# A decoder layer on one core: the 8 x 128 maxima of each attention head turned by the array's transposition, where a float32 product with the identity turned them

## The chip, the cores and the metric

The kernel runs on one core of one Trainium2 chip. The metric is the time of one execution on the device in microseconds (us). Three runs of the kernel before gave 1570.14, 1571.79 and 1575.17 us. A further execution was profiled, and its rows are what is quoted here.

## What is computed

A post-norm decoder layer on x of shape (4, 1024, 256), all in float32. The parts, in order: an autocorrelation attention, a cross attention to 64 context rows, and a feed-forward part that is itself a self-attention with 16 heads of width 16 and a mixture of 8 experts. The change lies in that self-attention:

```python
        attn = jnp.einsum('bhnd,bhmd->bhnm', q, k) * (1.0 / np.sqrt(DK))
        attn = jax.nn.softmax(attn, axis=-1)
        y = jnp.einsum('bhnm,bhmd->bhnd', attn, v)
```

with n and m running over 1024 tokens, 4 batches and 16 heads, so 64 heads in all.

## The kernel before

The stage of the change is `project_and_attend`. It projects q, k and v, and then goes through 64 heads in slots, software-pipelined: in slot s four things of four heads are in flight.

- `a(k)`, eight a slot, for head s: scores of 128 queries against all 1024 keys, queries on the partitions (L307). VectorE takes their maxima, one `TENSOR_REDUCE` for each k (L548), into `sb_m_mx`, 128 partitions x 8.
- `maxima()`, once a slot, for head s - 1: the 128 x 8 maxima are turned to 8 x 128 in a PSUM bank (L364). ScalarE copies them out (L483), GpSimd splits them into three bf16 parts (L228 to L232), and the sync queue's DMA puts these as three further rows under q (L181), so that the next product subtracts the maxima by itself.
- `b(m, h)`, sixteen a slot, for head s - 2: scores again with keys on the partitions, maxima subtracted (L336). ScalarE takes the exponential of each (L470).
- `products(m0, lag)`, four a slot: exponentials times v and a column of ones (L351, float32).
- `results()`, once a slot, for head s - 3: the result is turned back (L377).

Nearly all of this is written for quarters of the array. The stationary operand has 32 columns, and four such products, for PSUM partitions 0, 32, 64 and 96, stand one after another in the code. In the trace such a product reads `96*32`, `99*32` or `128*32` (rows * columns of the stationary operand), and a product on the whole array reads `128*128`. Below, the quarter of PSUM partitions 0 to 31 is called the first quarter. The maxima are `128*8` and go to PSUM partitions 0 to 7, so to the first quarter alone.

The order within a slot is written out by hand. Around the change it is:

```python
                a(0), b(0, 0), b(0, 1), a(1), b(1, 0)
                products(6, 3)
                maxima()
                b(1, 1), b(2, 0), a(2), a(3), b(2, 1), b(3, 0)
                products(0, 2)
```

Slots 0 and 1 are different. They hold the last batch's projections (L259 and L273, on the whole array, `128*128`) between the `a(k)`, and in slot 1 `maxima()` stands after `a(2)` and ahead of an L273. From slot 2 to slot 63 every slot is full. Slot 64 and those behind it have no `a(k)` any more.

A float32 product stands in the trace as two pairs of a weight load (`PEld`) and a `MATMUL`, a bf16 product as one pair. The kernel already has other float32 transpositions on the whole array (`pe.transpose` in L245, L1306, L2433 and elsewhere).

Of the kernel before, what the change touches and what calls it, by code (L numbers as in the profile page):

```python
# [18 lines left out]
P = 128  # L19
TPB = S // P  # L20
# [21 lines left out]
def project_and_attend(nc, ctx, t, dram):  # L42
# [8 lines left out]
    def sb(name, shape, dt=F32):  # L51
        return ctx.enter_context(nc.sbuf_tensor("sb_m_" + name, shape, dt))

    def sem(name):
        return ctx.enter_context(nc.semaphore("m_" + name))
# [7 lines left out]
    ps, pz, ident, v_all, y_all = t["ps"], t["pz"], t["ident"], t["v_all"], t["y_all"]  # L63
# [7 lines left out]
    mx = sb("mx", [P, 2, TPB])  # L71
# [24 lines left out]
    def v_ready(b):  # L96
# [5 lines left out]
    set_up, v_in, scores1, maxed, mxT_done, mxT_read, split_done = (sem(n) for n in (  # L102
        "set_up", "v_in", "scores1", "maxed", "mxT_done", "mxT_read", "split_done"))
# [11 lines left out]
    def rotating(use):  # L115
        return 4 + ROTATION.index(use) % 3

    def maxima_bank(s):

        return ps[7] if s == 1 else ps[rotating("mxT")]  # L120
# [14 lines left out]
    with nc.Block() as block:  # L135
# [101 lines left out]
        def _(pe):  # L237
# [51 lines left out]
            def slot(s, par, it, edge):  # L289
# [66 lines left out]
                def maxima():  # L356
                    if not after:
                        return
                    pe.wait_ge(maxed, TPB * s)
                    if two:  # L360
                        pe.wait_ge(exped, W * e + FREE["mxT"])
                    elif s == 1:
                        pe.wait_ge(rest_done, U * B)
                    pe.matmul(maxima_bank(s)[0:TPB, 0:P], mx[:, (par - 1) % 2, :],  # L364
                              ident[:, :], start=True, stop=True).then_inc(mxT_done, 1)

                def results():
                    if not three:
# [20 lines left out]
                if s == 1:  # L389
                    for k in range(TPB):  # L390
                        values(B - 1, k)
                        a(k)
                        if k == 2:
                            maxima()
                    return
# [5 lines that stand above are left out]
# [2277 lines left out]
```

## Time and profile before

| what | value |
|---|---|
| time, three runs | 1570.14, 1571.79, 1575.17 us |
| the profiled execution: its time / span of its profile | 1574.36 / 1572.4 us |
| TensorE busy (share of the span) | 1501.7 us (96%) |
| VectorE busy | 1134.4 us (72%) |
| ScalarE busy | 879.7 us (56%) |
| GpSimd busy | 379.6 us (24%) |
| granted TensorE clock, mean | 0.986 |
| first and last maxima turned (L364) | at 468.4 and 1165.8 us of the span |

The span is the time from the first to the last instruction in the profile, and the execution's own time is 2.0 us longer. "PE busy" counts a matmul from its start to its modelled end, and neighbouring matmuls overlap, so the step from one start to the next tells more than the duration of one.

### The profile page before, as it was taken

The numbers are of one execution on the slowest core, as the hardware profiler recorded it, in microseconds if no ns is written. First come the engines' busy times: TensorE is split into PE (matmuls) and PEld (weight loads), VectorE is DVE, ScalarE is ACT, GpSimd is POOL, SyncE is SP. The second block draws the span as 40 slices with busy tenths as digits, with TensorE's granted clock in tenths as the row PEclk, the third lists the DMA queues.
The fourth block names the chain that finished last, engine by engine and source line by source line (L and its number), as shares of the span: only waits on it lengthen the run. The fifth ranks groups of instructions, "written<-read, shape, count | busy, mean of one in ns | idle before, by whom it ended". The sixth has DMA issues, their size and how long they took to land. (4 is left out here: it accounts for less than half of the span.)

```text
span 1572.4 us, 45249 instructions
## 1 busy us (share of the span) xinstructions
PE 1501.7 (96%) x18762; PEld 1107.1 (70%) x18762; DVE 1134.4 (72%) x1703; ACT 879.7 (56%) x1608; POOL 379.6 (24%) x604
## 2 busy tenths in 40 slices
PE   7999999978899999999999999999998999999997
PEld 4656677655445666666666666666657889999997
DVE  5787798876868898988889898988855633333332
ACT  2223666654447888888888888888884311111111
POOL 4110332223431111111111111111111125454443
PEclk9999999998999999999999999999999989999999
DMA  6000000002341111111111111111105945656552
GB/s 203 1 21 11 11 2 2 2 1 78 107 159 42 43 35 43 36 41 38 39 39 38 41 36 43 35 42 37 39 13 157 284 161 204 201 194 212 186 214 67
DMA packets 80082, 124.12 MB, mean 79 GB/s; under 512 B 22243, under 2 KB 46949, under 8 KB 79878
## 3 DMA queue, kind: packets, MB, share of 16 engines
q1 hardware_dynamic: 74262, 105.87, 22.3%
q0 software_dynamic: 5616, 15.34, 2.6%
q8 instruction: 151, 2.47, 0.7%
q14 instruction: 53, 0.43, 0.1%
HBM read 94.66 MB, written 26.08 MB: 77 GB/s over the span
## 5 line engine op out<-in xcount | busy, mean ns | idle before, releaser
L548 DVE TENSOR_REDUCE sb_m_mx<-banks 128x1 f32<-128x1024 f32 x512 | 603.5, 1219 | 76.6 <-PE banks L307 68.7
L470 ACT ACTIVATE sb_m_pT<-banks 128x512 f32<-128x512 f32 x1024 | 556.4, 595 | 110.4 <-PE banks L336 99.4
L336 PE MATMUL banks<-sb_m_q,sb_m_k 99*32 99x512 bf16 x4096 | 467.2, 380 | 2.1 <-DMA sb_m_q<-sb_m_mx_parts 1.2
L307 PE MATMUL banks<-sb_m_k,sb_m_q 96*32 96x512 bf16 x4096 | 360.1, 379 | 0.8 <-DVE sb_m_mx L548 0.5
L351 PE MATMUL banks<-sb_m_pT,sb_m_v 128*32 128x256 f32 x4096 | 314.8, 378 | 0.7 <-ACT sb_m_pT L470 0.7
L336 PEld LDWEIGHTS banks<-sb_m_q,sb_m_k 99*32 99x32 bf16 x4096 | 178.0, 95 | 81.0 <-ACT sb_m_pT L470 6.1
L351 PEld LDWEIGHTS banks<-sb_m_pT,sb_m_v 128*32 128x32 f32 x4096 | 176.2, 109 | 59.8 <-ACT sb_m_pT L470 1.2
L307 PEld LDWEIGHTS banks<-sb_m_k,sb_m_q 96*32 96x32 bf16 x4096 | 158.5, 96 | 76.3 <-DVE sb_m_mx L548 5.6
L2484 ACT ACTIVATE sb_e_hT<-banks 128x512 f32<-128x512 f32 x78 | 46.6, 597 | 236.8 <-PE banks L2442 236.8
L228 POOL CAST sb_m_mx_parts<-sb_m_mxT 8x128 bf16<-8x128 f32 x64 | 18.1, 284 | 574.4 <-issue 563.5
L2442 PEld LDWEIGHTS banks<-sb_e_xT,w 128*128 128x128 f32 x1248 | 145.3, 192 | 3.4 <-DVE sb_e_xT L2494 1.5
L2442 PE MATMUL banks<-sb_e_xT,w 128*128 128x128 f32 x1248 | 145.8, 275 | 1.1 <-DVE sb_e_xT L2494 1.1
L2459 PE MATMUL banks<-w,sb_e_hT 128*128 x624 | 141.2, 379 | 0.6 <-DVE sb_e_x L2501 0.6
L2459 PEld LDWEIGHTS banks<-w,sb_e_hT 128*128 128x128 f32 x624 | 115.5, 190 | 15.1 <-issue 1.0
L2501 DVE TENSOR_TENSOR sb_e_x<-sb_e_x,banks 128x256 f32<-128x256 f32 x39 | 16.4, 421 | 106.8 <-PE banks L2459 106.8
L2494 DVE TENSOR_SCALAR sb_e_xT<-banks,table_ln_w,table_ln_b 128x128 f32<-128x128 f32 x78 | 28.4, 406 | 56.5 <-PE banks L2433 56.5
L1453 DVE RECIPROCAL sb_b_rec<-banks 128x256 f32<-128x256 f32 x32 | 56.1, 1754 | 16.5 <-PE banks L1317 16.1
L780 PE MATMUL banks<-sb_w_qk,sb_xfT 128*128 128x512 f32 x128 | 57.3, 596 | 0.8 <-ACT sb_xfT L889 0.8
L377 PE MATMUL banks<-ident_sb,sb_m_y_raw 128*32 128x128 f32 x1024 | 56.9, 278 | 0.5 <-ACT sb_m_y_raw L478 0.5
L2405 POOL DMA_INDIRECT out_x<-sb_e_y,token_to x39 | 40.6, 1040 | 51.1 <-DVE sb_e_y L2515 49.6
L1407 ACT ACTIVATE sb_b_prT<-banks 128x1024 f32<-128x1024 f32 x32 | 32.8, 1023 | 33.4 <-PE banks L1306 33.4
L1240 POOL TENSOR_TENSOR X<-sb_b_xs,cross_bo 128x256 f32<-128x256 f32 x32 | 23.0, 726 | 96.2 <-ACT sb_b_xs L1367 96.2
(251 smaller groups left out, 1969.1 us busy)
## 6 DMA issues: line engine op xcount, KB each, us to landing
w<-in_w SPq DMA_DIRECT2D x47, 1024.0 KB, 5.2
sb_m_q<-q_parts SPq DMA_DIRECT2D x384, 32.0 KB, 1.8
sb_m_k<-k_parts SPq DMA_DIRECT2D x384, 32.0 KB, 1.8
q_parts<-sb_m_parts SPq DMA_DIRECT2D x24, 256.0 KB, 2.4
k_parts<-sb_m_parts SPq DMA_DIRECT2D x24, 256.0 KB, 2.4
X<-in_x SPq DMA_DIRECT2D x4, 1024.0 KB, 10.1
x_rows<-X SPq DMA_DIRECT2D x8, 512.0 KB, 8.3
z_rows<-sb_g_zs SPq DMA_DIRECT2D x8, 512.0 KB, 4.4
```

Of the source, the lines that this page charges most:

```text
L307: mm = pe.matmul(ps[2 * (k % 2) + h][c:c + 32, :], q_s[0:R, i, k * P + c:k * P + c + 32], k_s[0:R, i, h * 512:(h + 1) * 512], start=True, ...
L336: mm = pe.matmul(ps[rotating(use)][c:c + 32, :], k_s[:, i2, m * P + c:m * P + c + 32], q_s[:, i2, h * 512:(h + 1) * 512], start=True, stop ...
L351: mm = pe.matmul(ps[7][32 * j:32 * j + 32, 0:256], v_s[:, par2, m, :], pT[:, m, j * 256:(j + 1) * 256], start=(m == 0), stop=(m == TPB - 1 ...
L377: tr = pe.matmul(ps[rotating("yT")][c:c + 32, r * P:(r + 1) * P], y_raw[:, r * P + c:r * P + c + 32], ident[:, :], start=True, stop=True, ...
L470: act.activation(pT[:, m, h * 512:(h + 1) * 512], ps[rotating(f"b{m}{h}")][:, :], ACT.Exp).then_inc(exped, 1)
L548: dve.tensor_reduce(mx[:, par % 2, k:k + 1], pz[:, 2 * (k % 2):2 * (k % 2) + 2, :].rearrange("p q n -> p (q n)"), AX.X, ALU.max).then_inc( ...
L780: mm = pe.matmul(bank[:, :], xfT[:, k, r, q * P:(q + 1) * P], w_qk[:, k, :], start=(k == 0), stop=(k == KT - 1 and f != 3))
L1453: dve.reciprocal(rec[:, :], ps[6][:, D:2 * D]).then_inc(rec_done, 1)
L2405: pool.indirect_dma_start(dram["out"], rows(token_to, j), y[:, j % W, :], None).then_inc(stored[j % W], 16)
L2442: mm = pe.matmul(ps[2 * q + m // 4][:, m % 4 * P:(m % 4 + 1) * P], w1[:, q, k, m * P:(m + 1) * P], xT[:, q, k, :], start=(k == 0), stop=(k ...
L2459: mm = pe.matmul(ps[6][:, 0:D], hT[:, q, m, :], w2[:, ds(e, 1), m, :].rearrange("p o n -> p (o n)"), start=(m == 0), stop=(m == HT - 1))
L2484: act.activation(hT[:, q, 4 * h:4 * h + 4, :], ps[2 * q + h][:, :].rearrange("p (m n) -> p m n", m=4), ACT.Gelu_apprx_tanh).then_inc(h_cop ...
```

## The change

```diff
                     elif s == 1:
                         pe.wait_ge(rest_done, U * B)
-                    pe.matmul(maxima_bank(s)[0:TPB, 0:P], mx[:, (par - 1) % 2, :],
-                              ident[:, :], start=True, stop=True).then_inc(mxT_done, 1)
+                    pe.transpose(maxima_bank(s)[0:TPB, 0:P], mx[:, (par - 1) % 2, :], ident[:, :]).then_inc(mxT_done, 1)
```

`mx[:, (par - 1) % 2, :]` (128 x 8) is the stationary operand and `ident` (128 x 128) the moving one in both forms. Bank, waits and the signal `mxT_done` stay, and so does the order of all instructions on all engines. Two things differ in the program as it is compiled. Where the product becomes two pairs of load and matmul, the transposition becomes one pair, so TensorE has 64 loads and 64 matmuls fewer. And the field that says which quarters of the array's columns an instruction addresses names the first quarter in both pairs of the product, and all four quarters in the pair of the transposition. The number of active columns is 8 in both. The instructions around it (L351 ahead, L336 behind) name one quarter each, as before.

## Rows read from the trace of the kernel before

**Rows 1.** The page: busy time of the engines, and 40 slices of the span.
```profile
PE 1501.7 (96%) x18762; PEld 1107.1 (70%) x18762; DVE 1134.4 (72%) x1703; ACT 879.7 (56%) x1608; POOL 379.6 (24%) x604
...
PE   7999999978899999999999999999998999999997
...
PEclk9999999998999999999999999999999989999999
```

**Rows 2.** Busy time of each engine from 480 to 1155 us (slots 2 to 63).
```profile
core 0: us, PE busy (x) PEld busy (x) DVE busy (x) ACT busy (x) POOL busy (x), PEclk, DMA share, GB/s
480.00:1155.00 675.00, 674.89 (x12798) 462.41 (x12798) 605.16 (x609) 558.21 (x1099) 99.76 (x305) 1.00 0.16 39
```

**Rows 3.** Who waited for whom from 480 to 1155 us: total, times, longest.
```profile
ACT sb_m_pT L470 <- PE banks L336: 95.4, 244, 0.6
DVE sb_m_mx L548 <- PE banks L307: 57.6, 124, 0.8
...
PEld banks L336 <- ACT sb_m_pT L470: 1.1, 3, 0.4
PEld banks L307 <- DVE sb_m_mx L548: 0.9, 5, 0.3
```

**Rows 4.** Timeline of PE, slots 2 and 63: start us, length us, what, count.
```profile
480.13 0.38 PE L364 MATMUL banks<-ident_sb,sb_m_mx 128*8 128x128 f32 x2
...
1155.01 0.27 PE L364 MATMUL banks<-ident_sb,sb_m_mx 128*8 128x128 f32 x1
```

**Rows 5.** Timeline of PE in mid-slot: sixteen quarter products of float32.
```profile
806.03 1.22 PE L351 MATMUL banks<-sb_m_pT,sb_m_v 128*32 128x256 f32 x16
```

**Rows 6.** Timeline of PE around the maxima of one slot.
```profile
800.58 0.59 PE L351 MATMUL banks<-sb_m_pT,sb_m_v 128*32 128x256 f32 x5
800.84 0.39 PE L336 MATMUL banks<-sb_m_q,sb_m_k 99*32 99x512 bf16 x3
801.01 0.38 PE L364 MATMUL banks<-ident_sb,sb_m_mx 128*8 128x128 f32 x2
801.13 0.48 PE L336 MATMUL banks<-sb_m_q,sb_m_k 99*32 99x512 bf16 x4
```

**Rows 7.** The instructions of L364: count, duration ns min/median/max.
```profile
L364 PEld LDWEIGHTS banks<-ident_sb,sb_m_mx x128: 85/90/92, 468.2 to 1165.6; 128*8 128x8 f32 x128
L364 PE MATMUL banks<-ident_sb,sb_m_mx x128: 269/273/274, 468.4 to 1165.8; 128*8 128x128 f32 x128
```

**Rows 8.** The instructions of L2433, a transposition on the whole array (78 calls).
```profile
L2433 PEld LDWEIGHTS banks<-ident_sb,sb_e_z x78: 140/142/145, 1278.9 to 1549.6; 128*128 128x128 f32 x78
L2433 PE MATMUL banks<-ident_sb,sb_e_z x78: 272/273/273, 1279.0 to 1549.7; 128*128 128x128 f32 x78
```

**Rows 9.** Timeline of PE: two transpositions of L2433 and what follows.
```profile
1296.06 0.38 PE L2433 MATMUL banks<-ident_sb,sb_e_z 128*128 128x128 f32 x2
1296.28 0.60 PE L2459 MATMUL banks<-w,sb_e_hT 128*128 x2
```

**Rows 10.** Timeline of PE in slot 1: whole array, quarters, whole array.
```profile
463.45 0.81 PE L273 MATMUL banks<-w_qkv,vblk_mem 128*128 128x256 f32 x3
464.19 0.61 PE L307 MATMUL banks<-sb_m_k,sb_m_q 96*32 96x512 bf16 x8
464.73 0.70 PE L273 MATMUL banks<-w_qkv,vblk_mem 128*128 128x256 f32 x2
```

**Rows 11.** Timeline of PE in slot 1, around its maxima.
```profile
468.19 0.39 PE L307 MATMUL banks<-sb_m_k,sb_m_q 96*32 96x512 bf16 x4
468.41 0.38 PE L364 MATMUL banks<-ident_sb,sb_m_mx 128*8 128x128 f32 x2
468.72 0.70 PE L273 MATMUL banks<-w_qkv,vblk_mem 128*128 128x256 f32 x2
```

**Rows 12.** Timeline of PE in slot 64, and a part of slots 64 to 67.
```profile
1165.64 0.27 PE L364 MATMUL banks<-ident_sb,sb_m_mx 128*8 128x128 f32 x1
...
1166.00:1190.00 24.00, 21.04 (x329) 11.66 (x324) 1.49 (x6) 19.06 (x36) 1.63 (x5) 1.00 0.07 15
```

## The prediction

> **What bounds the kernel now.** I read the page first, then the windows by engine, the waits and the timeline of the stage. Over the span TensorE is busy 96% at nearly the full clock, and VectorE, next to it, 72% [rows 1]. The stage of the change runs from about 468 to 1190 us. In its steady part, 480 to 1155 us, TensorE is busy 674.89 of 675.00 us at a granted clock of 1.00, VectorE 605.16, ScalarE 558.21 [rows 2]. The waits say the same from the other side: ScalarE and VectorE wait 95.4 and 57.6 us for TensorE's scores there, while TensorE's loads wait 1.1 and 0.9 us for them [rows 3]. A slot is as long as what TensorE has to stream. The maxima of slot 2 start at 480.13 and those of slot 63 at 1155.01 us [rows 4], so a slot takes 674.88 / 61 = 11.06 us. VectorE fills 90% and ScalarE 83% of it, 9.9 and 9.1 us.
>
> A busy share hides that the array works as four quarters side by side. Sixteen quarter products of 256 float32 columns start within 1.22 - 0.38 = 0.84 us [rows 5], 0.056 us from one start to the next, where whole-array products of the same size take (0.81 - 0.38) / 2 = 0.215 us each [rows 10]. Each quarter therefore has its own chain of steps of about 0.215 us. The maxima belong to the first quarter alone, and the trace shows that quarter as the last one. In one slot [rows 6], the five L351 end with the first quarter's, which starts at 800.58 + 0.59 - 0.38 = 800.79 us. Three of the next four L336, those of the other quarters, start already at 800.84, ahead of the maxima at 801.01. The fourth, the first quarter's, is the last of the group that begins at 801.13, so it starts at 801.13 + 0.48 - 0.38 = 801.23. So the first quarter goes from its L351 to its next L336 in 0.43 us, namely 0.22 for the L351 and 0.11 for each of the two passes of L364. The others don't pay for the maxima. The slot has the length of the first quarter's chain.
>
> **The change part by part.**
>
> *One pass in place of two.* 64 calls of L364 give 128 matmuls [rows 7], while 78 calls of a float32 transposition give 78 [rows 8]. A pass of the transposition is no shorter: both last 273 ns at the median [rows 7, 8], two transpositions take 1296.28 - 1296.06 = 0.22 us [rows 9], and two passes of L364 take 0.22 as well [rows 6]. The chain of the first quarter loses one pass, 0.11 us.
>
> *From quarters to the whole array and back.* The compiled transposition addresses all four quarters, though only 8 columns are active. So in each slot TensorE goes from quarter products (L351) to a whole-array instruction and back to quarter products (L336), which it never does now between slots 2 and 63. Slot 1 shows the price of both turns [rows 10]. From whole to quarters: three L273 start at 463.45, 463.67 and 463.88, and the L307 at 464.19. That is 0.31 us in place of 0.22, so 0.09 extra. From quarters to whole: the second four L307 start at 464.19 + 0.61 - 0.38 - 0.01 = 464.41, and the L273 at 464.73. That is 0.32 in place of 0.22, so 0.10 extra. There is a third part: a load directly behind a turn has nothing to hide under. Behind the turn the second L273 starts 0.70 - 0.38 = 0.32 us after the first, where 0.215 is usual. That exposes 0.10 us for a load of 128 float32 columns that belongs to a product of two passes. Behind the turn to quarters, eight L307 of 32 bf16 columns lie within 0.61 us where 0.38 + 0.215 + 0.01 = 0.605 would be usual, so up to 0.01 is exposed there.
>
> What the load of 8 columns costs when nothing hides it, no row shows. It lies between nothing and the 0.10 of 128 columns. I take it as nothing, because in width it is nearest to the 32 columns with their 0.01, and because it is the shortest load of these in the trace (90 ns, against 142 for 128 columns) [rows 7, 8].
>
> The Trainium skill has a rule for this, in "TensorEngine Tiling (Array Packing)", section "Key Properties": a change of the tiling mode drains TensorE. Its section "Gotcha 2: Feature Incompatibilities" adds that column tiling excludes the transpose mode for float32 input on trn2. By that rule the change could not stay in a quarter, and the sum would be the one below; slot 1 agrees with the drain, with 0.09 and 0.10 us.
>
> *The sum of a slot.* Before: 0.22 + 0.11 + 0.11 = 0.43 us in the first quarter from its L351 to its L336 (0.01 of it is rounding). After: 0.32 (L351 with the turn to the whole array) + 0.11 (one pass) + 0.09 (the turn back) + 0.01 (the L336's exposed load) = 0.53 us, now for all four quarters. The three others, which did this stretch without the maxima, end up level with the first, which was behind them. The rest of the slot stays, and a slot becomes 11.06 + 0.10 = 11.16 us.
>
> *How many.* Slots 2 to 63 are 62 slots: 62 x 0.10 = 6.2 us. In slot 1 the maxima stand between L307 (quarters) and L273 (whole) [rows 11], so the turn is there already and only moves ahead of them. One pass goes (0.11), and the L273's load, exposed until now by 0.10, can lie under the transposition. That is -0.2 us. In slot 64 nothing changes: from 1166 us TensorE is busy 21.04 of 24 us and has room [rows 12].
>
> *What else could move.* The maxima are ready in PSUM at about the same moment: the pass that signals starts 0.33 us after the first quarter's L351 now, and 0.32 us after it then, and both last 273 ns. ScalarE, GpSimd and the three DMAs behind them get them in time as before. VectorE and ScalarE gain 0.10 us of room in a slot. The L336 of the three other quarters, which now start early, start later by (801.23 + 0.10) - 800.84 = 0.49 us. But a bank is handed to ScalarE by the signal on the last of the four quarters, and ScalarE waits 95.4 us for L336 already. What it loses here lies in front of its own spare 17% of the slot.
>
> *The total.* 6.2 - 0.2 = +6.0 us. The profiled execution took 1574.36 us with a span of 1572.4, so it would become 1580.4 with a span of 1578.4. The median of the three runs is 2.6 us below that execution, and from it the forecast is 1571.8 + 6.0 = **1577.8 us**, 0.38% slower. A measurement of this kernel can tell about 0.3%, or 4.7 us, from no change. The forecast is just over it.
>
> **The rivals.**
>
> *Faster: the transposition doesn't hold up the other quarters.* If an instruction with 8 active columns is put into the first quarter whatever its field says, there is no turn, and the first quarter loses one pass. That gives 63 x 0.11 = 6.9 us less, **1564.9 us**. The Trainium skill, "Perfetto Trace Analysis", section "Transposes", says to use the transposition and not an ordinary matmul wherever something is to be transposed. For this rival speak the halved passes and that TensorE has no gap to lose. Against it speak slot 1, where both turns cost, and the compiled field. It decides where the two turns together cost less than 0.11 us; rows show 0.19. Chance 0.12.
>
> *Much slower: the exposed load is priced as for the L273.* If the load of the transposition behind the drain costs 0.10 us as it does there, a slot is 0.20 us longer: 62 x 0.20 = 12.4, less 0.2, gives **1584.0 us**. For it speaks that the fixed part of a load is most of its duration (90 ns for 8 columns, 142 for 128), against it the L307's load of 32 columns, whose exposure was 0.01. Chance 0.10.
>
> *No change that can be told.* The turn is cheaper behind L351 than behind L307, or a part of it lies in the lag between the quarters, and 0 to 0.07 us a slot is left: **1574 us**, somewhere between 1571.8 and 1576.2. For it speaks that the whole effect is small; against it that both turns cost about the same whichever line stood ahead (0.20 us from the second L364 pass to the L273 in slot 1, which is a pass of 0.11 and 0.09 [rows 11]). Chance 0.06 as a case of its own.
>
> **How the numbers follow.** The likeliest case, both turns paid and the load hidden or nearly so, has 0.72. Its own range is 1575.5 to 1580.5 us (0.06 to 0.14 us a slot), and I count 0.61 of it beyond 0.3% and 0.11 within. Slower: 0.61 + 0.10 = 0.71. Same: 0.11 + 0.06, rounded to 0.16. Faster: 0.12, rounded to 0.13. The range runs from 1570.5, where a slot loses nothing, to 1584.5 us, where the load is fully exposed; the faster rival lies outside it, and little else.
>
> **What would show it in the changed profile.** One matmul and one load of L364 for each head, 64 each. The start-to-start time of the maxima in the steady part: 11.16 us if I am right, 10.95 for the faster rival, 11.26 for the much slower. Around them, no L336 of the next group ahead of the maxima, all four L336 within a few ns, and the four quarters level with each other through the slot. The step from the last L351 to the transposition 0.32 us, and from it to the L336 0.20. TensorE still busy without a gap from 480 us on. The prediction would be wrong if the L336 of the other quarters still started ahead of the transposition, or if the waits showed TensorE waiting for ScalarE or VectorE in the steady part, which would mean that the quarters' lag had covered something.

## The result and the profile after

The changed kernel took 1577.60 us (median of 11 runs, 1575.31 to 1580.43), the kernel before 1571.24 us (median of 11 runs, 1566.39 to 1575.17). The ratio is 1.0043, with a 95% interval from 1.0031 to 1.0055: 6.4 us, or 0.4%, slower. The forecast was 1577.8 us. All runs in this document had a granted clock of 0.98 or more over the span, but for one of the ten of e9 (2211.97 us at a clock of 0.656), which is counted in that median and left out of its ratio.

The page of the changed kernel, busy times and slices as in [rows 1]:
```profile
PE 1505.6 (96%) x18698; PEld 989.4 (63%) x18698; DVE 1135.4 (72%) x1703; ACT 886.2 (56%) x1608; POOL 379.7 (24%) x604
...
PE   7999999978899999999999999999998999999997
...
PEclk9999999999999999999999999999999989999999
```
There are 64 matmuls and 64 loads fewer, and TensorE is still the engine that is full. The busy time of the loads fell by 118 us, though only 64 of 18762 are gone. Busy time counts the time in which at least one load runs. Before, the loads of the first quarter and those of the three others lay at different moments. Now they lie on top of one another.

The window from 480 to 1155 us, as in [rows 2]:
```profile
480.00:1155.00 675.00, 675.00 (x12632) 344.14 (x12636) 599.44 (x605) 558.99 (x1089) 99.80 (x305) 1.00 0.16 39
```
The clock is the same, and 12632 matmuls fit into it where 12798 did. VectorE's busy time fell by 5.7 us with the pace.

The waits in it, as in [rows 3]:
```profile
ACT sb_m_pT L469 <- PE banks L336: 95.0, 244, 0.7
DVE sb_m_mx L547 <- PE banks L307: 63.4, 123, 1.0
PEld banks L364 <- issue: 24.7, 60, 0.4
...
PEld banks L336 <- ACT sb_m_pT L469: 0.8, 2, 0.4
```
The new line is the load of the transposition: 60 times it came 0.41 us after the end of the load before it, with nothing that the profile could name to wait for ("issue"). This is how the turn shows in the waits. The loads behind it don't run ahead of it either:
```profile
791.85 0.09 PEld L364 LDWEIGHTS banks<-ident_sb,sb_m_mx 128*8 128x8 f32 x1 [0.41 <-issue]
792.05 0.12 PEld L336 LDWEIGHTS banks<-sb_m_q,sb_m_k 99*32 99x32 bf16 x8
```
In the kernel before, three loads of L336 stood level with the first load of L364:
```profile
800.80 0.09 PEld L364 LDWEIGHTS banks<-ident_sb,sb_m_mx 128*8 128x8 f32 x1
800.80 0.10 PEld L336 LDWEIGHTS banks<-sb_m_q,sb_m_k 99*32 99x32 bf16 x3
```

The timeline around the maxima, as in [rows 4] and [rows 6]:
```profile
479.09 0.27 PE L364 MATMUL banks<-ident_sb,sb_m_mx 128*8 128x128 f32 x1
...
790.88 1.04 PE L351 MATMUL banks<-sb_m_pT,sb_m_v 128*32 128x256 f32 x16
791.85 0.27 PE L364 MATMUL banks<-ident_sb,sb_m_mx 128*8 128x128 f32 x1
792.05 0.62 PE L336 MATMUL banks<-sb_m_q,sb_m_k 99*32 99x512 bf16 x8
...
1160.51 0.28 PE L364 MATMUL banks<-ident_sb,sb_m_mx 128*8 128x128 f32 x1
```
The sixteen L351 lie in 1.04 us where those of [rows 5] needed 1.22, since all four quarters now start each step together: the last four start at 790.88 + 1.04 - 0.38 - 0.01 = 791.53. From there to the transposition it is 0.32 us, and from it to the first L336 0.20. In none of the slots 3 to 63 does an L336 stand between the last L351 and the transposition any more. From slot 2 to slot 63 it is (1160.51 - 479.09) / 61 = 11.17 us a slot, and 11.06 before.

In slot 1, as in [rows 11]:
```profile
466.93 0.62 PE L307 MATMUL banks<-sb_m_k,sb_m_q 96*32 96x512 bf16 x8
467.48 0.27 PE L364 MATMUL banks<-ident_sb,sb_m_mx 128*8 128x128 f32 x1
467.59 0.60 PE L273 MATMUL banks<-w_qkv,vblk_mem 128*128 128x256 f32 x2
```
From the last L307 (466.93 + 0.62 - 0.39 = 467.16) to the second L273 (467.59 + 0.22 = 467.81) it is 0.65 us, where it was 0.85 (468.19 to 469.04). Here the turn was paid anyway, and the change gains 0.20 us.

The two profiled executions differ by less than the medians, 3.5 us in the span. The stage accounts for more than that, and 0.9 us came back ahead of the first maxima (468.4 against 467.5) and 2.1 us behind the last (406.8 us to the end of the span against 404.6). No instruction differs there, but the granted clock does. From 350 to 400 us, before and changed:
```profile
350.00:400.00 50.00, 41.92 (x162) 25.36 (x163) 33.12 (x99) 19.55 (x25) 15.96 (x12) 0.86 0.17 64
350.00:400.00 50.00, 39.41 (x164) 22.90 (x165) 34.10 (x101) 21.35 (x27) 16.79 (x13) 0.97 0.17 64
```
Over the whole span it is 0.986 and 0.989. This can be why single executions of one kernel differ (those of the kernel before by up to 8.8 us); no run isolates it. In the slots the clock is 1.00 in both, and there the growth is close to that of the medians (6.4 us): 6.5 us from slot 2 to slot 63, less the 0.20 of slot 1.

### The profile page after: what moved, and what is told of

It reads as the page before. It is cut to its first block and busy times, and to the rows that moved or that the text cites. A ratio compares the mean times of both kernels' runs of the same rounds, so it can differ in the third digit from the quotient of the medians.

```text
span 1575.9 us, 45121 instructions
## 1 busy us (share of the span) xinstructions
PE 1505.6 (96%) x18698; PEld 989.4 (63%) x18698; DVE 1135.4 (72%) x1703; ACT 886.2 (56%) x1608; POOL 379.7 (24%) x604
## 5 line engine op out<-in xcount | busy, mean ns | idle before, releaser
L336 PE MATMUL banks<-sb_m_q,sb_m_k 99*32 99x512 bf16 x4096 | 333.1, 381 | 2.4 <-DMA sb_m_q<-sb_m_mx_parts 1.3
L307 PE MATMUL banks<-sb_m_k,sb_m_q 96*32 96x512 bf16 x4096 | 287.9, 379 | 0.9 <-DVE sb_m_mx L547 0.5
L351 PE MATMUL banks<-sb_m_pT,sb_m_v 128*32 128x256 f32 x4096 | 265.6, 379 | 0.7 <-ACT sb_m_pT L469 0.7
L351 PEld LDWEIGHTS banks<-sb_m_pT,sb_m_v 128*32 128x32 f32 x4096 | 121.2, 110 | 104.3 <-ACT sb_m_pT L469 1.2
L307 PEld LDWEIGHTS banks<-sb_m_k,sb_m_q 96*32 96x32 bf16 x4096 | 106.1, 97 | 113.9 <-DVE sb_m_mx L547 5.0
L336 PEld LDWEIGHTS banks<-sb_m_q,sb_m_k 99*32 99x32 bf16 x4096 | 101.7, 96 | 105.1 <-ACT sb_m_pT L469 5.9
L901 ACT ACTIVATE sb_qk<-banks 128x512 f32<-128x512 f32 x32 | 19.1, 597 | 47.2 <-PE banks L779 38.7
```

The source lines that it names most:

```text
L307: mm = pe.matmul(ps[2 * (k % 2) + h][c:c + 32, :], q_s[0:R, i, k * P + c:k * P + c + 32], k_s[0:R, i, h * 512:(h + 1) * 512], start=True, ...
L336: mm = pe.matmul(ps[rotating(use)][c:c + 32, :], k_s[:, i2, m * P + c:m * P + c + 32], q_s[:, i2, h * 512:(h + 1) * 512], start=True, stop ...
L351: mm = pe.matmul(ps[7][32 * j:32 * j + 32, 0:256], v_s[:, par2, m, :], pT[:, m, j * 256:(j + 1) * 256], start=(m == 0), stop=(m == TPB - 1 ...
```

## The experiments

The measure of each experiment is the length of a slot: the time from one head's maxima to the next head's. All are stated against 11.06 us (before) and 11.17 us (changed). The table has the median and the mean of the 61 times from slot 2 to slot 63 in each kernel's trace, counted at the pass that signals. Under "expected" stand the values of the rival accounts, in the order of the recorded text. Each ratio is to runs of the kernel before made together with the experiment's, whose medians were 1570.97 to 1572.09 us.

| kernel | starts in slots 2 and 63, us | slot, mean | slot, median | expected | time, median us | ratio to before (95%) |
|---|---|---|---|---|---|---|
| before | 480.24, 1155.12 | 11.06 | 11.061 | | 1571.24 | |
| changed | 479.09, 1160.51 | 11.17 | 11.167 | 11.16 | 1577.60 | 1.0043 (1.0031 to 1.0055) |
| e1_two_together | 479.88, 1168.40 | 11.29 | 11.279 | 11.28 or 11.48 | 1586.80 | 1.0093 (1.0070 to 1.0117) |
| e2_two_apart | 478.38, 1178.67 | 11.48 | 11.481 | 11.48 or 11.28 | 1598.36 | 1.0164 (1.0128 to 1.0200) |
| e3_wide_turn | 478.57, 1162.88 | 11.22 | 11.214 | 11.22 or 11.17 | 1580.22 | 1.0054 (1.0034 to 1.0073) |
| e4_wide_product | 477.90, 1172.13 | 11.38 | 11.385 | 11.37 or 11.06 | 1593.84 | 1.0135 (1.0095 to 1.0175) |
| e5_bf16_maxima | 478.24, 1145.08 | 10.93 | 10.898 | 10.90 or 11.06 | 1562.02 | 0.9941 (0.9922 to 0.9959) |
| e6_quarters_in_turn | 478.67, 1150.41 | 11.01 | 10.957 | 10.90 or 11.06 | 1567.76 | 0.9971 (0.9960 to 0.9982) |
| e7_results_turned | 478.70, 1156.33 | 11.11 | 11.105 | 11.10 or 10.84 | 1572.71 | 1.0015 (1.0002 to 1.0027) |
| e8_bf16_in_turn | 477.48, 1144.88 | 10.94 | 10.929 | 10.86, 10.88 or 10.90 | 1562.81 | 0.9953 (0.9936 to 0.9970) |
| e9_last_quarter | 479.10, 1154.55 | 11.07 | 11.070 | 11.06, or up to 0.2 more | 1573.36 | 1.0009 (0.9996 to 1.0023) |

### e1: a second transposition beside the first

```diff
+                    if two:
+                        pe.transpose(maxima_bank(s)[0:TPB, P:2 * P], ident[:, 0:TPB], ident[:, :])
                     pe.transpose(maxima_bank(s)[0:TPB, 0:P], mx[:, (par - 1) % 2, :], ident[:, :]).then_inc(mxT_done, 1)
```
Expected:

> The changed kernel with a second transposition of the same shape (the identity's first 8 columns, into an unused part of the same bank) directly ahead of that of the maxima, in slots 2 to 64. The second result is used by nobody. The slot is 11.17 us long in the changed kernel. If the price is that of a turn to the whole array and back, paid once for each stretch of whole-array work, the slot grows by one pass alone: 0.11 us, to 11.28 us. If each transposition carries its own extra of 0.2 us, it grows by 0.3 us, to 11.48 us.

Measured: 11.28 us a slot. The timeline shows where the 0.11 us are:
```profile
806.84 0.27 PE L365 MATMUL banks<-ident_sb 128*8 128x128 f32 x1
806.95 0.27 PE L366 MATMUL banks<-ident_sb,sb_m_mx 128*8 128x128 f32 x1
807.15 0.40 PE L336 MATMUL banks<-sb_m_q,sb_m_k 99*32 99x512 bf16 x4
```
The second one follows after 0.11 us, a bare pass, and the step to the L336 is 0.20 us behind it. A transposition has no extra of its own. What costs is the way in and the way out, once. The first of the two is also the one whose 8-column load has nothing to hide under, and its step of 0.11 us (0.109 to 0.112 in 61 slots) has no room for an exposed load.

### e2: a second transposition away from the first

```diff
+                    if use == "b21":
+                        pe.transpose(ps[rotating(use)][0:TPB, 0:P], ident[:, 0:TPB], ident[:, :])
                     for c in range(0, P, 32):
                         mm = pe.matmul(ps[rotating(use)][c:c + 32, :], k_s[:, i2, m * P + c:m * P + c + 32],
```
Expected:

> The changed kernel with the same second transposition, but apart from the first: between the quarter products L307 of a(3) and the quarter products L336 of b(2, 1), into a bank that these overwrite. If the turn is what costs, it is paid a second time: 0.32 + 0.11 + 0.09 + 0.01 - 0.22 = 0.31 us, so the slot is 11.48 us long and the time 19 us above the changed kernel's, about 1597 us. If the extra of the change came from levelling the four quarters, which is done once a slot already, only the pass is added: 11.28 us and about 1584 us.

Measured: 11.48 us a slot and 1598.36 us. This is the same instruction as in e1, and it costs 0.31 us here where it cost 0.11 there. Its surroundings:
```profile
812.21 0.82 PE L307 MATMUL banks<-sb_m_k,sb_m_q 96*32 96x512 bf16 x12
812.96 0.27 PE L336 MATMUL banks<-ident_sb 128*8 128x128 f32 x1
813.17 0.40 PE L338 MATMUL banks<-sb_m_q,sb_m_k 99*32 99x512 bf16 x4
```
The last L307 start at 812.21 + 0.82 - 0.38 - 0.01 = 812.64, so it is 0.32 us in and 0.21 us out. The quarters were already level there, and the price came all the same. So the loss is not the levelling.

### e3: the load of the transposition made 128 columns wide

```diff
-    mx = sb("mx", [P, 2, TPB])
+    mx = sb("mx", [P, 2, P])
...
-                    pe.transpose(maxima_bank(s)[0:TPB, 0:P], mx[:, (par - 1) % 2, :], ident[:, :]).then_inc(mxT_done, 1)
+                    pe.transpose(maxima_bank(s)[:, 0:P], mx[:, (par - 1) % 2, :], ident[:, :]).then_inc(mxT_done, 1)
...
+                    dve.memset(mx[:, :, :], 0.0)
```
Expected:

> The changed kernel with the maxima in a tile of 128 columns, the other 120 set to zero once, and all 128 turned. Field, turn and number of passes stay those of the changed kernel, only the weight load has 128 columns in place of 8. If the exposed load goes with its columns, the slot grows by 0.05 us (the first transposition of L1306 behind a wait is followed by the second after 0.16 us where 0.11 is usual), to 11.22 us. If the load behind a turn has a fixed price or none, the slot stays at 11.17 us.

Measured: 11.21 us a slot, 0.05 more than with 8 columns.
```profile
804.05 0.33 PE L364 MATMUL banks<-ident_sb,sb_m_mx 128*128 128x128 f32 x1
804.31 0.62 PE L336 MATMUL banks<-sb_m_q,sb_m_k 99*32 99x512 bf16 x8
```
The transposition lasts 0.33 us in place of 0.27, and the L336 follow after 0.26 in place of 0.20. An exposed load goes with its columns: 120 columns more make 0.05 us by the slot and 0.06 by this step. By the same rate the 8 columns of the change cost nothing that can be seen, as the step of 0.11 us in e1 shows directly. That was the disputed term.

### e4: the old product, but on the whole array

```diff
-    mx = sb("mx", [P, 2, TPB])
+    mx = sb("mx", [P, 2, P])
...
-                    pe.matmul(maxima_bank(s)[0:TPB, 0:P], mx[:, (par - 1) % 2, :],
+                    pe.matmul(maxima_bank(s)[:, 0:P], mx[:, (par - 1) % 2, :],
...
+                    dve.memset(mx[:, :, :], 0.0)
```
Expected:

> The kernel before, its float32 product with the identity kept, but with the maxima in a tile of 128 columns of which 120 are zero, so that the product stands on the whole array. No transposition is in it. If the turn belongs to the whole-array instruction whatever it computes, the first quarter's 0.43 us become 0.32 + 0.10 (exposed load of 128 columns and two passes) + 0.11 + 0.11 + 0.09 + 0.01 = 0.74 us and the slot 11.37 us. If the drain belongs to the transposition as an operation, the slot stays at 11.06 us.

Measured: 11.38 us a slot, 0.32 more than before, with no transposition in the kernel.
```profile
807.63 0.49 PE L364 MATMUL banks<-ident_sb,sb_m_mx 128*128 128x128 f32 x2
808.04 0.40 PE L336 MATMUL banks<-sb_m_q,sb_m_k 99*32 99x512 bf16 x4
```
The two passes start 0.21 us apart (0.49 - 0.28), of which 0.10 is the exposed load, and the L336 follow 0.20 behind the second. So the turn belongs to the step between quarters and the whole array, not to the transposition as an operation. With a turn in both, one pass and a narrow load (the changed kernel) are 0.21 us better than two passes and a wide one (this kernel), and with a wide load in both (e3) it is still 0.17. The gain that the change offers is real where the array stands whole already.

### e5: one pass without a turn

```diff
-    mx = sb("mx", [P, 2, TPB])
+    mx = sb("mx", [P, 2, TPB], BF16)
+    ident_b = sb("ident_b", [P, P], BF16)
...
                     pe.matmul(maxima_bank(s)[0:TPB, 0:P], mx[:, (par - 1) % 2, :],
-                              ident[:, :], start=True, stop=True).then_inc(mxT_done, 1)
+                              ident_b[:, :], start=True, stop=True).then_inc(mxT_done, 1)
...
+                    dve.tensor_copy(ident_b[:, :], ident[:, :]).then_inc(set_up, 1)
```
Expected:

> The kernel before with the maxima written as bfloat16 by the reduction and turned by a product with a bfloat16 identity, still in the first quarter. The softmax subtracts the rounded maximum from numerator and denominator alike, so what is computed stays the softmax; only the value that is subtracted is rounded. One bf16 pass of 128 columns takes 0.055 us (a quarter of the 0.215 of 512 columns) where the two float32 passes take 0.22. If the first quarter's chain sets the slot, it shrinks by 0.16 us to 10.90 us, and the time by about 10 us to 1561 us. If the slot is set by something common to the quarters, it stays at 11.06 us.

Measured: 10.90 us a slot at the median (one slot of 12.76 us lifts the mean to 10.93), and 1562.02 us. The ratio is 0.9941, with an interval from 0.9922 to 0.9959.
```profile
796.04 0.39 PE L337 MATMUL banks<-sb_m_q,sb_m_k 99*32 99x512 bf16 x3
796.18 0.22 PE L365 MATMUL banks<-sb_m_ident_b,sb_m_mx 128*8 128x128 bf16 x1
796.24 0.46 PE L337 MATMUL banks<-sb_m_q,sb_m_k 99*32 99x512 bf16 x4
```
The maxima take the first quarter 0.06 us (796.24 - 796.18, where the first of the four is the first quarter's), and three quarters still run ahead. This is the version that beats both kernels: it puts one pass of 0.055 us in the place of two of 0.11 and leaves the array in quarters. VectorE is nearer now: from 480 to 1150 us the loads of L308 wait 7.9 us for its maxima, where they waited 0.9 before. At a slot of 10.90 us, the full gain forecast, this has cost nothing that can be seen.

### e6 and e9: the same product in other quarters

```diff
-                    pe.matmul(maxima_bank(s)[0:TPB, 0:P], mx[:, (par - 1) % 2, :],
+                    pe.matmul(maxima_bank(s)[32 * par:32 * par + TPB, 0:P], mx[:, (par - 1) % 2, :],
...
-                    act.activation(mxT[:, :], maxima_bank(s)[0:TPB, 0:P], ACT.Identity).then_inc(mxT_read, 1)
+                    act.activation(mxT[:, :], maxima_bank(s)[32 * par:32 * par + TPB, 0:P], ACT.Identity).then_inc(mxT_read, 1)
```
This is e6; e9 has `96` in place of `32 * par`. Expected of e6:

> The kernel before with its float32 product unchanged, but put into another quarter in each slot (PSUM partitions 0, 32, 64, 96 in turn), so that over four slots each quarter carries one pair of passes. If each quarter runs its own chain and a lag lasts over slots, the slot is 0.22 x 3/4 = 0.16 us shorter, 10.90 us, and the time about 1561 us. If the quarter that is behind holds up the others within a slot, because signals and waits come with the last of the four, nothing is carried over and the slot stays at 11.06 us, the time at 1571 us. In both cases it isn't longer, since no turn is added.

Expected of e9:

> The kernel before with its float32 product unchanged, but always in the last quarter (PSUM partitions 96 to 103) in place of the first. If the slot is as long as the chain of the quarter that holds the maxima, whichever it is, it stays at 11.06 us and the time at 1571 us. With the quarters taken in turn TensorE's loads waited 12.9 us for exponentials, which they hardly do with the maxima in the first. A wait stands on the first of four quarter products. If such waits come when another quarter than the first is behind, they show here too, and the slot is longer than 11.06 us by what they cost, up to 0.2 us.

Measured: e9 has 11.07 us a slot, as before, and a ratio that can't be told from 1. So the slot is as long as the chain of the quarter that holds the maxima, whichever it is. e6 lies between its two theories. Its slots repeat in cycles of four, at the maxima 10.94, 11.02, 10.89 and 11.12 us. Their mean is 10.99 us (two long slots, of 11.72 and 11.42, lift that of all 61 to 11.01), so full levelling's 0.16 us came to 0.07, which is less than half. The time, 1567.76 us, is 4.3 us below the 1572.09 of the runs beside it, which fits. The four single lengths say little, because the pass is in another quarter each time: at ScalarE's L478 the same cycle reads 10.94, 11.03, 10.94 and 11.06. The waits of TensorE's loads show something that is all but absent before [rows 3]. In e6:
```profile
PEld banks L336 <- ACT sb_m_pT L470: 12.9, 46, 0.4
```
In e9:
```profile
PEld banks L336 <- ACT sb_m_pT L470: 9.6, 61, 0.4
```
When another quarter than the first is behind, the first arrives early at the waits, which all stand on its product. In e9 these 9.6 us cost next to nothing, since the first quarter isn't the late one there. In e6 it may be that they eat what is missing. The trace speaks for it: all 46 waits lie in the slots whose maxima are in the second, third or fourth quarter, and none in those with the first. That is an inference from the rows and was not tested.

### e8: both together

The edits of e5 and e6 in one kernel. Expected:

> The bf16 maxima (reduction writes bfloat16, product with a bfloat16 identity, one pass of 0.055 us) put into another quarter in each slot. Again what is computed stays the softmax, with a rounded value subtracted. If the quarters could be levelled over slots, the slot would shrink from the 10.90 us of the bf16 maxima in the first quarter by 0.055 x 3/4 = 0.04 us to 10.86 us, and the time by 2.6 us. With the float32 product only about half of such a gain came, because loads then waited for exponentials; with the same share the slot is 10.88 us. If all of it is lost, 10.90 us.

Measured: 10.93 us a slot at the median and 1562.81 us, no better than e5. The slot is 0.03 us longer at the median of the one trace of each, while the two times can't be told apart (ratios 0.9941 and 0.9953, with intervals that overlap). That missed all three of the expected values. The loads wait 17.5 us for exponentials from 480 to 1150 us here, against 0.2 in e5, and again never in a slot with the maxima in the first quarter. With a pass of 0.06 us there is little left to level, and it seems that the waits cost more than the levelling brings; no run separates the two.

### e7: the same exchange for the results of a head

```diff
-                        for c in range(0, P, 32):
-                            tr = pe.matmul(ps[rotating("yT")][c:c + 32, r * P:(r + 1) * P],
-                                           y_raw[:, r * P + c:r * P + c + 32], ident[:, :], start=True, stop=True,
-                                           skip_group_check=True)
+                        tr = pe.transpose(ps[rotating("yT")][:, r * P:(r + 1) * P],
+                                          y_raw[:, r * P:(r + 1) * P], ident[:, :])
```
Expected:

> The kernel before with its maxima untouched and the same exchange made at another place: the results of a head (L377), turned by 8 float32 products in quarters, four passes in each quarter, become 2 float32 transpositions of 128 x 128 on the whole array. In each quarter four passes go (0.44 us). By the steps seen with the 128 columns turned at once, a turn with its exposed load and one transposition adds 0.31 + 0.26 + 0.01 - 0.22 = 0.37 us, and the second transposition 0.11, together 0.48 us. If turn and passes are all, the slot is 0.04 us longer than before, 11.10 us, and the time about 1574 us. If halving the passes were what counts, it would be 0.22 us shorter, 10.84 us.

Measured: 11.105 us a slot and a ratio of 1.0015 (1.0002 to 1.0027). The four passes of each quarter (0.44 us) became a turn, an exposed load and two passes (0.48 us with the 0.22 of the step before counted off), by steps that are known from the runs above:
```profile
803.64 0.60 PE L336 MATMUL banks<-sb_m_q,sb_m_k 99*32 99x512 bf16 x3
804.17 0.44 PE L376 MATMUL banks<-ident_sb,sb_m_y_raw 128*128 128x128 f32 x2
804.54 0.40 PE L336 MATMUL banks<-sb_m_q,sb_m_k 99*32 99x512 bf16 x4
```
The two passes start 0.44 - 0.27 = 0.17 us apart, 0.06 more than a bare pass of 0.11, which is the exposed load, and the L336 follow 0.20 behind the second. The turns of e1 to e4 thus price an exchange at another place and of another size, to 0.01 us. Here the turn is nearly paid for, because the fullest quarter saves two passes (four become two) and not one.

## Why the prediction was right

**The bound.** That a slot is as long as TensorE's longest quarter was read from the 675 us without a gap. It held in every kernel: with one exception (e8) each was forecast from the length of a chain in a quarter, or bracketed by it (e6).

**One pass in place of two.** 64 pairs of load and matmul went, one a slot, and each pass takes 0.11 us of its quarter's chain. Where the array is whole already, in slot 1, the pass and the load that had been exposed gave 0.20 us, as forecast.

**The turn.** In steps it was forecast at 0.32 in, 0.11 for the pass and 0.09 out, with 0.01 behind it. The trace shows 0.32, then 0.20 for pass and way out together. The slot grew by 0.106 us at the median, forecast 0.10. e1 and e2 show that the turn is paid for each stretch on the whole array, and e4 that it belongs to the array's arrangement and not to the operation. No run transposes within a single quarter, so what that would cost isn't known.

**The exposed load.** Taken as nothing, with 0.10 us as the other end. e3 measured 0.05 for 128 columns of a transposition, so the 0.10 of the L273 would have been twice too much even for a wide load. The L273 is a float32 product of two passes, and e4 shows 0.10 for a wide load of that kind; why a product's load is exposed for longer than a transposition's stays open. For 8 columns nothing is left to see (e1). The much slower rival falls with it. The prediction had no row for this term and chose one end of its bounds; that end was the right one.

**The faster rival.** It needed the transposition to stay in the first quarter, and there is no L336 ahead of it any more. Its premise, that a pass out of the first quarter is worth its full length, was right, and e5 collects it: 0.16 us a slot.

**The others.** ScalarE waits for L336 as before (95.0 against 95.4 us) and VectorE waits longer (63.4 against 57.6). Nothing behind the maxima became late. The total was forecast at +6.0 us; the medians say +6.4.

**The luck in it.** That the forecast lies 0.2 us from the measured median is in part chance. Its base, the median of three runs, was 0.6 us above that of eleven, and its rise was 0.4 us too small, so the two errors nearly cancel. What tests the mechanism is the slot, with 0.106 us where 0.10 was forecast, and the steps around the maxima. The lower end of the range, 1570.5 us, was called the case in which a slot loses nothing; by the sum that case is 1571.8 - 0.2 = 1571.6. Nothing hangs on it.

## What to carry to other kernels

Read a TensorE that is full by its quarters, not by its busy share: sixteen quarter products that start within 0.84 us are four chains, and the one with an instruction more is the length of the loop. Before exchanging an instruction among quarter products for one on the whole array, count the way in and out, here about 0.20 us together, against the passes it saves in the fullest quarter, here 0.11 us each (one saved pass lost 0.1 us a slot, two with a wide load lost 0.04 in e7); group such instructions so that one turn serves several. If a pass is to go, look first for a way to make it cheaper in place: bf16 maxima took 0.16 us out of each slot, and the softmax is the same whichever value near the maximum is subtracted.

## What the runs showed of the hardware that was not expected

The turn is very regular. In the six kernels that make it in every full slot (the changed one, e1 to e4 and e7) the way in took 0.31 to 0.32 us from the last quarter products' start (0.22 without a turn). The way out took 0.20 us from a pass of 0.11, behind a transposition as behind a product, and 0.26 where that pass's own load of 128 columns was exposed (e3). An exposed load costs by its columns and its kind: 0.05 to 0.06 us for 128 float32 columns that are turned, 0.10 for those of a two-pass product, and nothing visible for 8.

The quarters can run out of order against the code: in the kernel before, three L336 of other quarters start 0.17 us ahead of the L364 that precedes them [rows 6], but a lead is not kept freely over slots. Spreading the maxima over the quarters brought 0.07 us a slot of the 0.16 that the sum of each quarter's work says (e6), and with the shorter pass the slot was 0.03 us longer than without spreading (e8). What holds the rest back stays open; the waits of the first quarter's loads for exponentials are the candidate.
